# One row product moved behind the last chunk's second gate, one elementwise step moved ahead of two weight pieces

## The reference, cut to what matters

```
si = slot_input / denom                       # 512 slots x 512
gi = si @ Wih.T + bih ;  gh = S @ Whh.T + bhh # S: the 64 initial slots
r = sigmoid(i_r + h_r) ; z = sigmoid(i_z + h_z) ; n = tanh(i_n + r * h_n)
S_new = (1 - z) * n + z * S
q, k, v = S_new @ wq + bq, S_new @ wk + bk, S_new @ wv + bv
S_comm = softmax(q k^T * scale) @ v
y = layernorm(S_new + S_comm) * ln_g + ln_b
out = (alpha^T-weighted sums of (y @ wvp + bvp)) @ wo + bo
```

## Time and profile before

| | |
|---|---|
| median of the runs | 360.4 us |
| profiled execution, its own time | 362.36 us |
| its span, first to last instruction | 360.6 us |
| mean granted TensorE clock | 0.992 |
| TensorE matmul busy | 343.4 us, 95% |
| VectorE, ScalarE, GpSimd busy | 261.8, 185.6, 205.8 us |

### The profile page before, as it was taken

One profiled execution on the slowest core, in us unless ns is written; L12 is line 12 of the kernel. 1 busy time (PEld: TensorE's weight loads), 2 busy tenths in 40 slices (PEclk: granted clock), 3 DMA queues, 4 the chain that ended last, 5 costly groups with the idle time before them and its releaser, 6 DMA issues.

```text
span 360.6 us, 6908 instructions
## 1 busy us (share of the span) xinstructions
PE 343.4 (95%) x2256; PEld 278.3 (77%) x2256; DVE 261.8 (73%) x740; ACT 185.6 (51%) x376; POOL 205.8 (57%) x350
## 2 busy tenths in 40 slices
PE   8999999999999999999999999999999959999981
PEld 5476558899898888988998898877789745677760
DVE  5346987777688778788787787677945764767864
ACT  2350033657859659568567677476511346421541
POOL 5044055888677866866786686646636114242793
PEclk9999999999999999999999999999999989999998
DMA  7799755332323232221322200019500000002399
GB/s 279 231 354 393 261 161 167 119 95 82 103 73 118 61 101 76 84 93 61 111 66 60 87 3 2 2 11 361 193 0 2 0 0 0 2 0 88 116 379 351
DMA packets 40934, 42.78 MB, mean 119 GB/s; under 512 B 3246, under 2 KB 32046, under 8 KB 40899
## 3 DMA queue, kind: packets, MB, share of 16 engines
q1 hardware_dynamic: 39088, 40.41, 33.8%
q10 hardware_dynamic: 1522, 1.27, 1.1%
q0 software_dynamic: 288, 0.66, 0.6%
HBM read 32.18 MB, written 8.39 MB: 113 GB/s over the span
## 4 chain that ended last, share of the span: by engine, by line
PE 64%; DVE 14%; POOL 8%; issue 6%; ACT 4%; DMA 2%; DVEq 0%; SPq 0%; POOLq 0%; ACTq 0%
PE psum L383 13%; PE psum L384 11%; PE psum L385 11%; PE psum L1347 5%; PE psum L1507 4%; PE psum L1535 3%; PE psum L1756 2%; PE psum L1389 2%; PE psum L1664 2%; POOL X L534 2%; PE psum L1488 2%; PE psum L1570 1%; DVE W_hi L784 1%; POOL hT_lo L529 1%; DMA WvpT<-in_WvpT 1%
## 5 line engine op out<-in xcount | busy, mean ns | idle before, releaser
L383 PE MATMUL psum<-GW_hi,hT_hi 128*128 128x292 f32 (+1 forms) x256 | 79.0, 309 | 1.1 <-POOL GW_lo L516 1.0
L385 PE MATMUL psum<-GW_lo,hT_hi 128*128 128x292 f32 (+1 forms) x256 | 74.1, 289 | 0.0
L384 PE MATMUL psum<-GW_hi,hT_lo 128*128 128x292 f32 (+1 forms) x256 | 73.9, 289 | 0.0
L534 POOL TENSOR_TENSOR X<-X,th 128x512 f32<-128x512 f32 x32 | 38.3, 1196 | 31.4 <-ACT th L1156 31.4
L383 PEld LDWEIGHTS psum<-GW_hi,hT_hi 128*128 128x128 f32 x256 | 48.5, 189 | 2.9 <-issue 2.0
L529 POOL TENSOR_TENSOR hT_lo<-xT,hT_hi 128x512 fp32r<-128x512 f32 x32 | 43.4, 1357 | 12.4 <-ACT hT_hi L1112 12.4
L384 PEld LDWEIGHTS psum<-GW_hi,hT_lo 128*128 128x128 f32 x256 | 48.4, 189 | 0.2 <-issue 0.2
L385 PEld LDWEIGHTS psum<-GW_lo,hT_hi 128*128 128x128 f32 x256 | 48.1, 188 | 0.0
L383 PE MATMUL psum<-xhT_hi,w_hi 128*128 128x256 f32 x128 | 38.5, 301 | 0.1
L384 PE MATMUL psum<-xhT_hi,w_lo 128*128 128x256 f32 x128 | 36.1, 282 | 0.0
L385 PE MATMUL psum<-xhT_lo,w_hi 128*128 128x256 f32 x128 | 36.1, 282 | 0.0
(11 more groups left out here) (258 smaller groups left out, 882.2 us busy)
## 6 DMA issues: line engine op xcount, KB each, us to landing
X<-in_x SPq DMA_DIRECT2D x32, 256.0 KB, 3.5
xT<-in_xT SPq DMA_DIRECT2D x32, 256.0 KB, 2.8
out<-ost SPq DMA_DIRECT2D x32, 256.0 KB, 2.6
WhhT<-in_WhhT SPq DMA_DIRECT2D x1, 3072.0 KB, 13.4
WihT<-in_WihT SPq DMA_DIRECT2D x4, 768.0 KB, 8.4
Wo<-in_wo ACTq DMA_DIRECT2D x4, 256.0 KB, 4.3
WvpT<-in_WvpT SPq DMA_DIRECT2D x4, 256.0 KB, 5.0
WaT<-in_WaT SPq DMA_DIRECT2D x1, 1024.0 KB, 11.4
```

Of the source, the lines that this page charges most:

```text
L383: pe.matmul(out, w_hi, m_hi, start=start, stop=False)
L384: pe.matmul(out, w_lo, m_hi, start=False, stop=False)
L385: return pe.matmul(out, w_hi, m_lo, start=False, stop=stop)
L534: pool.tensor_tensor(tile_x(r), tile_x(r), halves(th[:, :]), ALU.add).then_inc(S("x2"), 1)
```

## The change

TensorE forms the row product after gate sum (3,2) and no longer before it, into bank 6 (`trX`) and not bank 0; so it first waits for `te`, and the wait for `bpb` moves from the query product to `values(1, ...)`. ScalarE copies the row after the tanh of the last candidate and not before it. GpSimd does `to_slots(0)` before low pieces 10 and 11, and VectorE does `new_slots(0)` before high pieces 10 and 11. No instruction is added or removed.

```diff
@@ -587,9 +587,12 @@
             pool.tensor_tensor(gd[:, c % 2, :].rearrange("p (b s) -> p b s", s=NS), bc(slotT[:, c, :], NB, 1),
                                gn[:, c % 2, :].rearrange("p (b s) -> p b s", s=NS), ALU.subtract).then_inc(S("gd"), 1)
 
-        for n in range(len(PIECES)):
+        for n in range(10):
             low_piece(n)
-        for c in range(KC):
+        to_slots(0)
+        low_piece(10)
+        low_piece(11)
+        for c in range(1, KC):
             to_slots(c)
 
         def scales_y(g):
@@ -950,9 +953,9 @@
         candidate_in(0)
         high_piece_of(9)
         gate_in(0, 1)
+        new_slots(0)
         high_piece_of(10)
         high_piece_of(11)
-        new_slots(0)
         for c in range(1, KC):
             gate_in(c, 0)
             candidate_own(c)
@@ -1298,9 +1301,9 @@
 
         last = KC - 1
         gate(last, 0)
+        candidate(last)
         act.wait_ge(S("bp_all"), 1)
-        act.copy(bpb[:, :], TURN).then_inc(S("bpb"), 1)
-        candidate(last)
+        act.copy(bpb[:, :], trX).then_inc(S("bpb"), 1)
         high_alpha(0)
         high_Wp(3)
         gate(last, 1)
@@ -1654,9 +1657,10 @@
         for gate in RUN_GATES:
             gate_sum(2, gate, 0, SLOTS)
         gate_sum(3, 0, 0, SLOTS)
+        gate_sum(3, 2, 0, SLOTS)
+        pe.wait_ge(S("te"), NPAIR)
         pe.wait_ge(S("bp"), 1 + KC)
-        pe.matmul(TURN, ones[:, :], rows[:, :], start=True, stop=True).then_inc(S("bp_all"), 1)
-        gate_sum(3, 2, 0, SLOTS)
+        pe.matmul(trX, ones[:, :], rows[:, :], start=True, stop=True).then_inc(S("bp_all"), 1)
         gate_sum(3, 1, 0, SLOTS)
 
         def product_of(W, bank, lo, hi):
@@ -1758,9 +1762,7 @@
                         last.then_inc(S("oc"), 1)
 
 
-        pe.wait_ge(S("te"), NPAIR)
         pe.wait_ge(S("in_qk"), 32)
-        pe.wait_ge(S("bpb"), 1)
         pe.wait_ge(S("snt"), KC - 1)
         product_of(Wq, banks[0], 0, KC - 1)
         product_of(Wk, banks[1], 0, KC - 1)
@@ -1773,6 +1775,7 @@
         pe.wait_ge(S("qkT"), 2)
         scores()
         values(0, 2, KC)
+        pe.wait_ge(S("bpb"), 1)
         values(1, 0, 2)
         values(2, 0, 2)
         weights_turned(0, 2, 1)
```

## The result

| | before | changed |
|---|---|---|
| median of 20 runs | 361.64 us | 359.42 us |
| lowest, highest | 359.87, 363.36 | 356.53, 362.05 |
| ratio | | 0.9927 (95%: 0.9899 to 0.9955) |
| profiled execution, its span | 362.36, 360.6 us | 359.84, 358.0 us |

The change makes the kernel faster by 0.73%, where 0.94% was forecast; the medians lie 2.2 us (0.61%) apart, since the ratio leaves out the run at 362.05 us, which counts as slow (over 1.5% above the fastest). The median is above the stated range, which ended at 358.9 us. The 20 runs of the changed kernel are in two groups that the mean granted clock of each run sorts without an exception: nine from 356.53 to 357.87 us with 0.992 to 0.996, eleven from 359.25 to 362.05 us with 0.987 to 0.989. (The mean is taken over the whole span, the low clock of the last slice included, so it is compared only within one order of the program.)

A forecast was written before the change was run, and what follows sets the result against it. TensorE, busy 95%, was held by its 3.65 us wait for `rows`; arriving 5.65 us early, then waiting 2.26 us for SnT, it gains 3.4 us: 360.4 - 3.4 = 357.0 us, range 355.8 to 358.9.

The forecast's parts named there:

- two signs of a wrong core: TensorE still waiting for `rows`, or SnT of chunk 3 not about 3 us earlier, would show the core wrong.
- Part 1: TensorE's gate sums and row product, then query and key: it reaches chunk 3's key product 5.65 us early, the ceiling.
- Part 2: GpSimd and VectorE ahead of `rows`: chunk steps come 1.37 us earlier, `rows` ready at 290.85, so no stall.
- give-back by GpSimd: Low piece 11 beside `candidate_own(1)` holds VectorE up, so chunk steps come 1.37 us earlier, not 2.23.
- lock rule: GpSimd and VectorE block each other for whole instructions; by it chunk steps come only 0.97 us earlier, whole sum 3.0 us.
- Part 3: Last chunk: ScalarE's list is late next; tanh of z comes 3.05 us earlier, SnT ends at 302.24, TensorE starts at 302.30.
- The sum: TensorE stands still 2.26 us for SnT; chunk 3's key product and all behind it come 3.4 us earlier.
- the chain's even passes: Query and key products before the change: 14 passes in 6.01 us without a gap, 0.43 us each.
- rival A: The clock falls in TensorE's new idle time, costing 1.7 us: gain 1.7, 358.7 us; chance 0.13.

The follow-up runs named there:

- e6: e5 with ScalarE's high_Wp(3) and high_Wp(0) moved behind high_values_weight(); ratio to the kernel before 0.9855, trace 355.41 us.
- e5: Changed kernel with ScalarE's tanh of z of the last chunk directly behind its candidate's tanh; ratio to the kernel before 0.9869, trace 355.50 us.
- e2: Kernel before with only to_slots(0) and new_slots(0) moved ahead of pieces 10 and 11, row product unmoved; ratio 0.9921, trace 360.94 us.
- e4: Changed kernel with values(0, 0, 2), four needed passes, moved ahead of TensorE's wait for the fourth SnT; ratio to the kernel before 0.9847.
- e1: Changed kernel with GpSimd's and VectorE's order of before, row product still behind gate sum (3,2); ratio to the kernel before 0.9941.
- e3_look2: Third trace of the changed kernel with 8 unneeded matmuls ahead of TensorE's wait for the fourth SnT; 359.55 us.
- e3_filler: Changed kernel with 8 unneeded matmuls ahead of TensorE's wait for the fourth SnT; ratio to the kernel before 0.9909, trace 357.71 us.
- e3_look1: Second trace of the changed kernel with 8 unneeded matmuls ahead of TensorE's wait for the fourth SnT; 357.85 us.

## Why the prediction was wrong, by its steps

The two signs of a wrong core that were named did not come: TensorE does not wait for `rows`, and SnT of chunk 3 is 3.2 us earlier (its end, 300.02 - 264.51 against 305.29 - 266.54).

**Part 1** held: no wait for `rows`, full clock from 288 to 300 us.

**Part 2** held to a tenth. From the cast, `gate_in(1,0)` came 2.35 us earlier (275.80 - 264.51 against 280.18 - 266.54; 2.23 forecast). `candidate_own(1)` took 1.65 us, and `rows` was ready 1.39 us earlier (1.37). The give-back by GpSimd was there. Of the lock rule (Trainium skill, "SBUF — State Buffer", section "Who interferes with whom") this case shows that one waits for the other, five times over (1.56, 1.65, 1.64, 1.74 and 2.17 us for operations of 0.69 and 1.23 us, 0.69 again once e6 moves the neighbour); its further 0.4 us, by which the chunk steps would come only 0.97 us earlier, the measured 1.39 speaks against.

**Part 3** named the right engine. The tanh of z came 3.24 us earlier (3.05 forecast): from start to start candidate and copy took 0.63 and 0.46 us (294.22, 294.85, 295.31), and I had 0.72 and 0.53. TensorE waited 1.92 us (2.26). e5 shows the cause: with the tanh of z first, the wait is 0.8 us.

**The sum without a fall**: 49.86 - 46.56 = **3.30 us**, against 3.4. The key product came 3.59 us sooner, and 0.29 of that was lost by the transposes behind it: after the idle time TensorE took 0.96 us to reach them (299.87 to 300.83) where I had two passes, 0.86, and before they had started at 306.38, sooner by 0.17 us than the chain's even passes put them.

**The step that failed is the clock behind the new wait.** The sum lets TensorE stand still for 2.26 us and go on at full clock. The opposite was rival A, "the clock falls in the new idle time", at 0.13, on the argument that 2.26 us lies nearer to the 1.1 us after which the clock had held. Its price was right (1.7 forecast, 1.67 measured); its chance was not: 11 of 20 runs by their mean clock, and seven of eight traces. Even 1.9 us can be followed by a fall. Two rows of one execution were read as two sides of a limit, when the runs show that the same wait goes either way, and that a longer one (e2, 2.3 us) was followed by a fall less often. With the chance as counted the expected gain is 3.30 - 0.55 x 1.67 = 2.4 us, 0.66%; measured were 0.73%, and 0.66% lies inside the interval.

**The other part of the miss is the baseline.** I set 357.0 from the median of three runs, 360.4 us. With the 361.64 us of 20 runs, the forecast gain of 3.4 would be 358.2 us, and 3.30 less the falls 359.3 us; 359.42 was measured. As a share, the forecast 0.94% lies inside the measured interval too (0.45 to 1.01%): the runs can't tell it from 0.66%, and it is the traces that show the missing 1.67 us. The profile I had lay 2 us above the median, and I took that as a constant: it was the slow front, which comes and goes.

## What to carry to other kernels

When a stall of TensorE is taken out, look for where the next one opens and cost it twice: its own length, and the clock behind it, as a case that comes with a probability. A gap of about 2 us is better filled with needed work that is ready (e4) or closed at the engine that makes it (e5) than left. And compare traces by the distance between two marks around the change, since the front of the program alone moved by 2.4 us between executions.

## What the runs showed of the hardware

- After an idle time of 3.6 us TensorE's clock was lower in both traces of the kernel before; after 1.9 to 2.0 us in seven of eight of the changed kernel; after 2.1 us (e1) and 2.3 us (e2) in the one trace of each, though nine of e2's twelve runs have a mean clock that leaves no room for a fall; after 0.8 us (e5), 0.2 us (e4, e3_look2) and none (e3_filler, e3_look1, e6) in no trace. Each fall in the middle lasted about 3.4 us (0.72 over six us); in the changed kernel, the only one traced with and without, it cost 1.67 us.
- The clock also falls ahead of the main loop: the product `psum<-encWT,WaT` took 9.69 us in two traces (e2, e3_look2) and 8.0 us in all others.
- A GpSimd operation that began only 0.07 us ahead held VectorE up by 1.05 us: SnT took 1.74 us when the rest of Wp began at 296.63 and SnT at 296.70 (e5), and 0.69 us when that work was moved away (e6).
